# Second softmax pass started one step earlier beside the first, in a token + attention + mixture-of-experts kernel on one core

## What is computed

```python
q, k, v = to_bh(q), to_bh(k), to_bh(v)                 # 4 sequences x 12 heads, width 16
attn = softmax(q @ k.T * scale)                        # first softmax, 512 x 512 per head
out  = attn @ v                                        # first weighted sum
out  = out @ proj_w.T + proj_b
sim_tokens = out / norm(out)                           # per head
sim  = sim_tokens @ sim_tokens.T * 10
sim  = where(sim < 0, -inf, sim)                       # the mask
sim  = softmax(sim)                                    # second softmax
out2 = sim @ v                                         # second weighted sum
h    = h + out2 @ proj_w.T + proj_b
```

## Time and profile before

| | before |
|---|---|
| median of 3 runs | 647.12 us |
| the three runs | 647.12, 639.49, 647.45 us |
| the profiled execution | 639.4 us, span 637.6 us |
| TensorE busy | 538.5 us (84%) |
| VectorE busy | 430.0 us (67%) |
| ScalarE busy | 341.5 us (54%) |
| GpSimd busy | 231.6 us (36%) |
| mean granted TensorE clock | 0.943 |

### The profile page before, as it was taken

One profiled execution on the slowest core, in us unless ns is written; L12 is line 12 of the kernel. 1 busy time (PEld: TensorE's weight loads), 2 busy tenths in 40 slices (PEclk: granted clock), 3 DMA queues, 4 the chain that ended last, 5 costly groups with the idle time before them and its releaser, 6 DMA issues.

```text
span 637.6 us, 11853 instructions
## 1 busy us (share of the span) xinstructions
PE 538.5 (84%) x3480; PEld 322.5 (51%) x3481; DVE 430.0 (67%) x859; ACT 341.5 (54%) x795; POOL 231.6 (36%) x281
## 2 busy tenths in 40 slices
PE   0658799988999899999998878426999999999990
PEld 0323323433344233533353332415999999999990
DVE  3489987888798999897678987376643434343420
ACT  1132676677788888788977856210333333334340
POOL 6860430417052150103113110003356666656541
PEclk9977999999999999999998999755999999999996
DMA  4182052135534180312333369822133232333321
GB/s 117 45 116 37 25 86 36 30 72 87 64 52 91 22 129 10 65 45 52 50 71 83 54 158 255 265 89 92 18 58 50 51 49 51 48 52 47 54 33 13
DMA packets 40562, 45.00 MB, mean 71 GB/s; under 512 B 10404, under 2 KB 34854, under 8 KB 40519
## 3 DMA queue, kind: packets, MB, share of 16 engines
q0 software_dynamic: 12864, 19.97, 18.5%
q1 hardware_dynamic: 27654, 24.52, 17.6%
HBM read 17.88 MB, written 7.60 MB: 40 GB/s over the span
## 4 chain that ended last, share of the span: by engine, by line
PE 63%; DVE 18%; issue 8%; DMA 6%; ACT 3%; POOL 0%; SPq 0%; POOLq 0%; DVEq 0%; ACTq 0%
PE psum L1121 11%; PE psum L973 10%; PE psum L1105 7%; DVE MX L745 5%; PE psum L1034 5%; PE psum L1010 5%; PE psum L1110 5%; PE psum L1041 4%; PE psum L1026 4%; DVE arena L759 4%; DMA result<-T,slot_dest 4%; PE psum L1063 3%; PE psum L998 2%; PE psum L1052 1%; ACT arena L596 1%
## 5 line engine op out<-in xcount | busy, mean ns | idle before, releaser
L596 ACT ACTIVATE arena<-psum 128x512 f32<-128x512 f32 x384 | 206.9, 615 | 42.5 <-PE psum L1034 27.5
L632 ACT ACTIVATE arena<-psum,b_sb 128x128 f32<-128x128 f32 x234 | 64.6, 375 | 127.2 <-PE psum L1110 127.2
L745 DVE TENSOR_REDUCE MX<-psum 128x1 f32<-128x512 f32 x192 | 123.4, 681 | 8.1 <-PE psum L1026 7.9
L759 DVE SCALAR_TENSOR_TENSOR arena<-arena 128x1024 f32<-128x1024 f32 x96 | 120.4, 1266 | 11.9 <-ACT arena L596 11.5
L973 PE MATMUL psum<-arena 128*17 128x512 f32 x768 | 102.0, 604 | 5.7 <-DVE arena L759 5.7
L511 POOL DMA_INDIRECT result<-T,slot_dest x39 | 68.6, 1759 | 73.8 <-DMA result<-T,slot_dest 50.9
L1121 PE MATMUL psum<-arena 128*128 x468 | 86.3, 335 | 0.0
L369 POOL DMA_DIRECT2D KS<-arena x72 | 36.8, 512 | 118.1 <-PE psum L1041 58.9
L1121 PEld LDWEIGHTS psum<-arena 128*128 128x128 f32 x468 | 75.0, 190 | 4.7
L1026 PE MATMUL psum<-late_stacks,arena 96*128 96x512 bf16 x144 | 57.5, 409 | 12.2 <-DMA late_stacks<-arena 7.3
L1041 PE MATMUL psum<-KS,QS 96*128 96x512 bf16 x192 | 66.4, 386 | 1.0 <-issue 0.5
(11 more groups left out here) (175 smaller groups left out, 643.0 us busy)
## 6 DMA issues: line engine op xcount, KB each, us to landing
late_stacks<-arena POOLq DMA_DIRECT2D x72, 64.0 KB, 4.3
QS<-arena SPq DMA_DIRECT2D x72, 64.0 KB, 3.6
KS<-arena POOLq DMA_DIRECT2D x72, 64.0 KB, 3.6
arena<-w SPq DMA_DIRECT2D x8, 576.0 KB, 8.1
arena<-arena SPq DMA_DIRECT2D x54, 64.0 KB, 4.4
arena<-w SPq DMA_DIRECT2D x8, 384.0 KB, 6.0
x_rows<-X SPq DMA_DIRECT2D x4, 384.0 KB, 2.5
result<-H SPq DMA_DIRECT2D x4, 384.0 KB, 3.1
```

What stands on the lines that cost most here:

```text
L596: act.activation((P1, P2)[ps][:, n % PRING, :], s, ACT.Exp, scale=(QSCALE, SIM_SCALE)[ps]).then_inc(done, 1)
L745: dve.tensor_reduce(MX[:, g % 2, CT * i + c:CT * i + c + 1], slot(k), AX_X, ALU.max).then_inc(freed[k % RING], 1)
L759: dve.scalar_tensor_tensor(p, p, 1.0, p, ALU.is_ge, ALU.mult).then_inc(masked, 1)
```

## The change

One number moves: the second softmax begins 53 steps after the first stage of its group instead of 54. All that is placed from OFF_E moves with it by one step: `sim_unit`, `mask`, the second `pv`, `save` and `normalise`, the loads `load_sim` where they aren't held by the first pass, and for each sequence the second output transpose, projection, norm and gate. The `pv` of the second softmax falls on odd steps now, at the same time and rank as that of the first; the sort is stable, so the second softmax's `pv` (of the lower group) stands first and the other right behind it.

```diff
-OFF_C, OFF_E = 11, 54
+OFF_C, OFF_E = 11, 53
```

## The result

| | before | after |
|---|---|---|
| median | 643.61 us (4 runs, 639.49 to 647.45) | 659.85 us (4 runs, 657.93 to 664.58) |
| ratio, with its 95% interval | 1 | 1.026 (1.016 to 1.037) |
| profiled execution: own time, span | 639.4, 637.6 us | 661.2, 659.5 us |
| mean granted TensorE clock | 0.943 | 0.928 |

The change makes the kernel slower by 16 us, 2.6%. That is clear of the spread of the runs; that it is more than 2% is not, as the interval begins at 1.6%. The forecast was 648.0 us with 636.5 to 658.5 around it; the result lies above the range.

A forecast was written before the change was run, and what follows sets the result against it. TensorE was taken to bound the three-stage steps by a hair, VectorE level. Terms -0.4 + 1.0 + 1.9 + 1.0 + 0.3 = +3.8 us on 639.4 gave 643.2; between two run levels, 648 us was named, range 636.5 to 658.5.

The forecast's parts named there:

- the sum for the three-stage part: Steps with both softmaxes and the first stage: 58 to 96 longer by 2 to 5 us, those to 107 within 1.
- The pairs: Two `pv` in a row, 27 times from step 57 to 109; TensorE gains 0.08 us a pair where it is the bound.
- The hole: Behind each pair TensorE gives readers no tile for 1.96 us; two clean steps take 4.85 for 4.78, +1.0 us in all.
- first sums' `save`: On ScalarE at odd steps, waiting for the pair's second `pv`: 0.8 us more, seven times, a third counted, +1.9 us.
- second sums' `save`: On ScalarE behind the hole, six times in the pairs' stretch: 0.5 us each, a third counted, +1.0 us.
- Second output part: Second output part, norm and gate move one step and keep their sizes; cost put at nothing.
- First loads: Operands of the first `sim_unit` may land late: a wait of 0 to 1.6 us once, 0.3 us taken.
- The clock: Rival: a stall shifted late in the attention or before the experts changes TensorE's clock, 2 to 4 us either way; chance 0.1.
- Starved readers: Rival: behind each pair VectorE and ScalarE run out of tiles, +13 us and more; sign: L1026 waits reach 10 us; chance 0.12.
- Packing: Rival: TensorE bounds clean steps, so its saved lead-in and a shorter second `pv` count in full, -2 to -6 us; chance 0.2.
- Pairs that don't meet: Rival: a late mask holds up the second softmax's `pv` and the first one's behind it, +8 us; chance 0.03.
- One step more of overlap: A two-stage step and a second-softmax step become one three-stage step: gain 0.4 us.

The follow-up runs named there:

- e3: Kernel before (offset 54) with the second softmax's `pv`, `save`, `normalise` and output part one step later, giving pairs: 645.70 us, 1.003.
- e17: Changed kernel with offset 55 and the second `pv`, `save` and `normalise` one step later, so no pairs: 641.42 us, 0.998 of the kernel before.
- e4: Changed kernel with offset 55 instead of 53, which also makes pairs: 652.77 us, 1.013 of the kernel before.
- e14: Changed kernel with the first sequence's second-score loads one step earlier and the first sums' `save` 0.7 step later: 658.17 us, 1.020 of before.
- e6: Changed kernel with the first softmax's `pv` half a step and its `save` 0.7 step later, opening the pairs: 655.99 us, 1.016 of before.
- e12: Changed kernel with first second-score loads a step earlier, second `pv`, `save`, `normalise` a step later, output part left early: 642.33 us, 0.996 of before.
- e1: Changed kernel with the first sequence's transposes and loads for the second scores one step earlier: 659.10 us, 1.024 of the kernel before.
- e10: Changed kernel with only the second sums' `normalise` one step later: 659.16 us, 1.022 of the kernel before.
- e11: Changed kernel with first second-score loads one step earlier and the second output part back where it stood: 658.88 us, 1.023 of before.
- e9: Changed kernel with first second-score loads a step earlier; second `pv`, `save`, `normalise` and output part back where they stood: 640.17 us, 0.994 of before.
- e2: Changed kernel with second `pv`, `save`, `normalise` and output part back where they stood, so no pairs: 642.58 us, 0.995 of the kernel before.
- e15: Changed kernel with first second-score loads one step earlier and `max_row` of groups 7 to 11 one step later: 667.05 us, 1.036 of before.
- e5: Changed kernel with offset 52 instead of 53, which makes no pairs: 653.02 us, 1.011 of the kernel before.
- e18: The changed kernel unaltered, run again for a second profile: 659.84 us, 1.026 of the kernel before.

## Why the prediction was wrong

**The step that failed** is the sum for the three-stage part: "Steps 58 to 96 become longer by 2 to 5 us, those to 107 stay within 1 us". Steps 57 to 106 grew by 13.2, about 8.2 by the order of work and 5.0 by the lower clock. The terms for the pairs came to 3.9 us, which is what pairs cost at another offset; two terms that were put at nothing are what failed: other work that meets the pairs (the second output part was written down as "Nothing"), and a lower clock inside this part. The rivals' weights were wrong with them.

*The pairs.* Twenty-seven, as forecast. Their length is 1.85 us, not 1.96: I had put the second `pv` at 0.98 and named 0.85 as the bound. It is 0.87, with the second one's weights loaded under the first. By the Trainium skill, "TensorE: Matmul & The Clock Gate", section "Step-by-step: what each phase is for", a load is pulled ahead of matmuls in flight when the row groups don't conflict or when it targets the background weight buffer; the trace agrees in that the load came 0.43 us ahead, and doesn't show which of the two held. I read the row of a load of another form behind a `pv` as if it spoke of all forms: it waits here as well (0.85 us at 249.32). TensorE's own sum for a pair was thus 0.11 us shorter than forecast, and that was still worth nothing.

*The hole.* ScalarE does stand behind the pairs, 1.2 us at 247 us where I had 0.8. Pairs at 54 cost 3.2 us (e3) and at 55 about 3.8 (e17 against e4); my terms for the hole and the two `save`s came to 3.9. That the size fits is luck in good part. The term for the first sums' `save` (1.9 us) is nothing, though its wait did grow (e14); the one for the second sums' `save`, 0.5 us each time, is 0.49 where it could be read, but I had taken a third of it. The periods with nothing else in them, which I costed at 0.07 us, go -0.14 (75), +0.25 (77) and +0.55 (101). And opening the pairs (e6) gave back only about 1 us, so the hole of 1.85 us as such is not shown to be the cause. What is shown to cost is that the second sums, with what follows them, come in the steps of the first ones: about 6 us at full clock (e12 against e1), of which the `normalise` alone is nothing (e10).

*Other work beside the pairs.* "Other work that happens to fall into the hole" stood in the prediction as its last doubt and had no price. By the order, 8.2 us are lost at 53 in place of 3.2 at 54. Single periods change by up to 2.2 us down (85) and 1.7 up (83). Of the 5.0 us between, up to 2.0 may be the second output part (next point; the two don't simply add, as e11 shows) and up to 1.5 the second sums' `save`.

*Second output part: "Nothing."* It costs 2.0 us without pairs (e12), 1.5 of them in steps 81 to 92. I had looked only at what waits for it, not at where its transposes and projections push those steps.

*First loads: 0.3 us, at most 1.6.* 3.6 us up to step 57 in this profile, of which e1 gives 3.1 back: the wait of 2.0, over the bound of 1.6, and behind it a stretch of lower clock which I had not connected with it. Taken away (e1 against the changed kernel, e9 against e2) it moves the ratio by 0.001 to 0.003, which the medians can't tell from nothing.

*The clock.* I gave the rival 0.1 and 2 to 4 us either way, outside the three-stage part. It came inside it, where the clock had been 1.00, and costs about 5.0 us there in this profile, some 1.6 behind the first loads, and perhaps part of the 4.5 us behind step 107. Of the three pieces between steps 53 and 106 only the first has a wait of 2 us right ahead of it. The Trainium skill, "Perfetto Trace Analysis", section "Matmul Optimizations", advises matmuls back to back in batches, since the engine scales its power by its use; I let it count for nothing as the clock was already full. Here batches went with less clock, 1.00 to 0.97.

*The rivals.* Starved readers, at +13 and more, came nearest in size, and of its sign VectorE's waits for L1026, 9.0 us, stand just under the 10 that I had named. But not by the mechanism as I put it, 0.5 us behind each of 27 pairs: at full clock the kernel with pairs at 54 loses 3.2, and TensorE's pair starved VectorE only here and there (0.5 to 0.9 us behind three pairs of steps 57 to 94). Packing is out: TensorE's saving of 27 x 0.11 us is real and buys nothing. Pairs that don't meet: out, the second sum starts 0.87 us after the first in every pair at full clock. One step more of overlap, costed at 0.4 us, is in e9, whose 0.6% is the most it can be, with the better loads in it.

*The base.* The 648 stood 4.4 us over the median of before as it came out (643.6), which hid a part of the miss: +3.8 us forecast, +16.2 measured. (The middle of the two levels 643.2 and 650.9 is 647, not 648, and the loop behind the 4.85 us sums to 4.82; neither changes the outcome.)

**What stays open.** Why the pairs cost 6.2 us of order at 53 (8.2 less the output part's 2.0) and 3.2 at 54 with the same neighbours one step away. Up to 1.5 of the 3.0 may be the second sums' `save`: with it moved, 63 and 79 take what they take in e3 (7.28 and 5.20). It isn't the `save` of the first sums or the `normalise` (e14, e10), and the early second scores cost nothing where there are no pairs (e2); e15 was to show it for the `max_row` and didn't. And why the clock falls at 298.8 us in one profile and not in the other. The stretch has no such piece in before, e2, e9, e12 and e17, and one to four in most kernels with pairs at 53 or 55. But e3 and e10 have pairs and none, and e5 has two and no pair, each by a single profile: it isn't a rule.

## What to carry to other kernels

Where TensorE feeds two readers through a short ring, spread the work that makes no tiles over the steps: two such pieces in a row saved TensorE 0.1 us here and stopped a reader for 1.2, and half a step between them helped little; a whole step did. When a change moves a whole chain by a step, cost the work that is carried along (here 2.0 us for an output part, 3.1 us for a first load), and then split the change: here keeping the offset, moving the sums and the output part back a step and the first loads forward gave a kernel 0.6% faster than before, out of one 2.6% slower. An order written by hand has coincidences of 1 to 2 us in a period of 5; a sum over typical steps doesn't find them, so a range for such a change must be wide on the slow side.

## What the runs showed of the hardware

- Two `pv` of the same form in a row: 0.87 us for the first, 0.97 for the one that a matmul of another form follows (248.35 to 249.32); weights of the second are loaded 0.43 us ahead.
- 6.8 us at the lower clock cost 3.3 us (after against e18), nearly all that half the clock can take (3.4), in a stretch where VectorE is as busy as TensorE. 3.4 us of it cost 1.6 in one place (e4 against e3, 11.02 and 9.38) and 0.8 in another (e18, steps 67 to 72).
- Where the clock is the same, a static order repeats itself to 0.07 us in a period of 4 to 9 us, and kernels with the same order in a stretch have the same times there (59,60: 7.81, 8.50). This makes single periods readable far under the 1% by which whole runs of a kernel differ.
- Part of that 1% comes from early on, as far as profiles show it: the first piece of lower clock, at 39 us, lasts 17.1 us in some profiles and 20.5 or 23.9 in others, and step 15 then starts at 77.0 to 78.6 us in place of 73.6 to 74.4.
